# Attention weights of two key blocks added by heads on GpSimd, one product with ones per pair, and the transfers of the normalisation issued by SyncE

## The reference, cut to what matters

```python
scores = jnp.einsum('bhqd,bhkd->bhqk', qn, kn) / jnp.sqrt(jnp.asarray(hd, x.dtype))
scores = jnp.where(causal, scores, jnp.finfo(scores.dtype).min)
w = jax.nn.softmax(scores, axis=-1)
a = jnp.einsum('bhqk,bhkd->bhqd', w, v)
```

## Time and profile before

| | us |
|---|---|
| median of 3 runs | 2458.92 (2458.35 to 2460.32) |
| profiled execution, its own time | 2456.73 |
| its span | 2454.6 |
| TensorE busy in the span | 2279.7 (93%) |
| attention stage, steady part | 487 to 1165 of the span, a unit every 47.3 |

### The profile page before, as it was taken

One profiled execution on the slowest core, in us unless ns is written; L12 is line 12 of the kernel. 1 busy time (PEld: TensorE's weight loads), 2 busy tenths in 40 slices (PEclk: granted clock), 3 DMA queues, 4 the chain that ended last, 5 costly groups with the idle time before them and its releaser, 6 DMA issues. The chain is left out here.

```text
span 2454.6 us, 32466 instructions
## 1 busy us (share of the span) xinstructions
PE 2279.7 (93%) x12520; PEld 1705.3 (69%) x12520; DVE 1165.7 (47%) x1799; ACT 793.3 (32%) x1671; POOL 728.3 (30%) x694
## 2 busy tenths in 40 slices
PE   6999992899999999999858799999999999999998
PEld 3777771666666666666446588888888888888887
DVE  5999994655555555555269611222222212121222
ACT  3333331255555555455435411111111111111111
POOL 2677674002112111111177122222222222222221
PEclk8999996699999999999989899999999999999999
DMA  6122224554465455443179511212121212111111
GB/s 223 69 103 90 98 98 120 122 128 117 102 149 126 106 135 139 111 102 89 37 244 308 204 48 52 69 48 69 52 69 49 68 53 68 44 58 49 48 56 52
DMA packets 161828, 243.70 MB, mean 99 GB/s; under 512 B 17124, under 2 KB 84292, under 8 KB 161184
## 3 DMA queue, kind: packets, MB, share of 16 engines
q1 hardware_dynamic: 153184, 220.66, 30.9%
q0 software_dynamic: 7456, 18.07, 2.5%
q10 hardware_dynamic: 1056, 3.15, 0.3%
HBM read 131.69 MB, written 59.26 MB: 78 GB/s over the span
## 5 line engine op out<-in xcount | busy, mean ns | idle before, releaser
L883 DVE TENSOR_REDUCE b_top<-b_psA 128x2 f32<-128x1024 f32 (+3 forms) x384 | 353.3, 954 | 246.0 <-PE b_psA L801 154.3
L950 ACT ACTIVATE b_probT<-b_psB 128x512 f32<-128x512 f32 (+3 forms) x768 | 338.7, 488 | 330.0 <-PE b_psB L825 242.3
L1313 DVE TENSOR_TENSOR f_gu<-f_psU,f_silu 128x512 f32<-128x512 f32 x128 | 88.5, 691 | 711.8 <-PE f_psU L1380 711.8
L1269 POOL TENSOR_SCALAR f_wd_hi<-f_wd 128x512 fp32r<-128x512 f32 x128 | 83.7, 654 | 822.5 <-PE f_psD L1365 775.6
L822 PE MATMUL b_psB<-b_stack 98*128 98x512 f32 (+3 forms) x768 | 268.2, 404 | 5.0 <-ACT b_probT L950 4.6
L801 PE MATMUL b_psA<-b_stack 96*128 96x512 f32 (+3 forms) x768 | 228.3, 387 | 30.2 <-DMA b_stack<-b_halves 20.3
L822 PEld LDWEIGHTS b_psB<-b_stack 98*128 98x128 f32 x768 | 140.6, 189 | 143.5 <-issue 99.8
L1289 ACT ACTIVATE f_silu<-f_psG 128x512 f32<-128x512 f32 x128 | 76.5, 598 | 503.8 <-PE f_psG L1380 503.8
L1378 PE MATMUL f_psG<-f_hT_hi,w_hi 128*128 128x512 f32 x512 | 200.2, 391 | 10.9 <-DVE f_hT_lo L1307 10.9
L1380 PE MATMUL f_psG<-f_hT_lo,w_hi 128*128 128x512 f32 x512 | 199.7, 390 | 0.0
L1379 PE MATMUL f_psG<-f_hT_hi,w_lo 128*128 128x512 f32 x512 | 199.7, 390 | 0.0
(11 more groups left out here) (177 smaller groups left out, 4136.2 us busy)
## 6 DMA issues: line engine op xcount, KB each, us to landing
b_stack<-b_halves SPq DMA_DIRECT2D x192, 256.0 KB, 5.1
f_wd<-in_wd_t SPq DMA_DIRECT2D x128, 256.0 KB, 2.6
qkv_d<-a_t SPq DMA_DIRECT2D x32, 512.0 KB, 2.7
b_land<-qkv_d SPq DMA_DIRECT2D x32, 512.0 KB, 4.6
a_x<-in_x SPq DMA_DIRECT2D x32, 256.0 KB, 3.2
qkv_d<-a_v SPq DMA_DIRECT2D x32, 256.0 KB, 3.0
b_v<-qkv_d SPq DMA_DIRECT2D x16, 512.0 KB, 5.9
att_d<-b_att SPq DMA_DIRECT2D x16, 512.0 KB, 3.2
```

Of the source, the lines that this page charges most:

```text
L883: dve.tensor_reduce(out, slot("score", NI * n + i)[:, :, 0:width], AX.X, ALU.max, negate=True).then_inc(s["maxed"], 1)
L950: act.activation(probT[:, (NW * n + w) % 3, j, 0:width], psB[:, i % 2, 0:width], ACT.Exp).then_inc(s["expd"], 1)
```

## The change

Per pair of blocks (0 and 1, 2 and 3, ...) GpSimd adds the second block's weights into the first's, head by head; TensorE then makes one product with ones per pair, three steps after the pair's second block was shifted. `b_probT` gets 5 buffers. The transfers of the normalisation move from GpSimd to SP, into the units after, as do the reciprocal (w = 8 to w = 0 of the next unit), the scaling (to w = 3 of the next unit, in two halves) and the store of b_att (from w = 10 of unit g+2 to w = 5 of unit g+3, for group g). Only this much of the diff matters for the order of the work:

```diff
+    PROBS = 5
+    def pair_at(k):
+        at = shift_at(k)
+        return (at[0], at[1] // 2) if at and at[1] % 2 == 1 else None
+    def sum_at(k):
+        return pair_at(k - 3)
+    def take_sum_at(k):
+        return take_at(k - 2)
...
+            def sums_out(n):
+                sp.wait_ge(s["taken_l"], 2 * n + 2)
+                sp.dma_start(scratch["sums"][0], sums[0:P:HD, n % 2]).then_inc(s["sums_out"], 16)
+            def few_in(n):
+                sp.wait_ge(s["sums_out"], 16 * n + 16)
...
+            def few_out(n):
+                sp.wait_ge(s["inverted"], n + 1)
...
+            def wide_in(n):
+                sp.wait_ge(s["few_out"], 16 * n + 16)
...
                 if w == 5 and 0 <= n < NG:
                     load_v(n)
-                if w == 10 and 0 <= n - 2 < NG:
-                    store(n - 2)
+                if 0 <= n - 2 < NG - 1:
+                    if w == 9:
+                        sums_out(n - 2)
+                    if w == 10:
+                        few_in(n - 2)
+                if 0 <= n - 3 < NG - 1:
+                    if w == 1:
+                        few_out(n - 3)
+                    if w == 2:
+                        wide_in(n - 3)
+                if w == 5 and 0 <= n - 3 < NG:
+                    store(n - 3)
...
+            def add_pair(n, i):
+                half, kb = BLOCKS[2 * i + 1]
+                width = (half + 1) * W - max(kb, half * HALF) * P
+                at = (NW * n + 2 * i) % PROBS
+                whole_at = (half + 1) * W - max(kb - 1, half * HALF) * P
+                pool.wait_ge(s["weighed"], NW * n + 2 * i + 1)
+                for j in range(4):
+                    into = probT[:, at, j, whole_at - width:whole_at]
+                    pool.wait_ge(s["expd"], 4 * (NW * n + 2 * i + 1) + j + 1)
+                    add = pool.tensor_tensor(into, into, probT[:, (at + 1) % PROBS, j, 0:width], ALU.add)
+                add.then_inc(s["added"], 1)
...
             for k in STEPS:
                 if prep_at(k):
                     high(*prep_at(k))
-                at = take_at(k)
-                if at and at[1] == 1 and at[0] < NG - 1:
-                    normalise(at[0])
+                if pair_at(k):
+                    add_pair(*pair_at(k))
+                n, w = unit(k)
+                if w == 3 and 0 <= n - 3 < NG - 1:
+                    normalise(n - 3)
...
+            def add_up(n, i):
+                half, kb = BLOCKS[2 * i]
+                pe.wait_ge(s["added"], NW // 2 * n + i + 1)
+                if kb == 0:
+                    at_least(pe, s["taken_l"], 2 * n + half)
...
                 if weigh_at(k):
-                    weigh(*weigh_at(k), False)
-                    weigh(*weigh_at(k), True)
+                    weigh(*weigh_at(k))
+                if sum_at(k):
+                    add_up(*sum_at(k))
...
                 if j == 0:
-                    at_least(act, s["summed"], NW * n + w - 2)
-                    at_least(act, s["weighed"], NW * n + w - 2)
+                    before = NW * n + w - PROBS
+                    if before % 2 == 0:
+                        at_least(act, s["summed"], before // 2 + 1)
+                    else:
+                        at_least(act, s["added"], before // 2 + 1)
+                        at_least(act, s["weighed"], before + 1)
```

More of the change, by code:

```diff
@@ L653, in attention_stage @@
         peak_rows = sb("b_peak_rows", [8 * TB, P])
-        probT = sb("b_probT", [P, 3, 4, W])
+        probT = sb("b_probT", [P, PROBS, 4, W])
         sums = sb("b_sums", [P, 2, C])
@@ L663, in attention_stage @@
         names = ("mask_in ln_ready whole ident_ready consts k_ones qk_in v_in turned hi_done lo_done scored maxed peaks_ready "
-                 "peaks_turned peaks_copied peaks_in shifted expd weighed summed taken_o taken_l sums_out few_in inverted few_out "
+                 "peaks_turned peaks_copied peaks_in shifted expd weighed added summed taken_o taken_l sums_out few_in inverted few_out "
                  "wide_in scaled end_inverted end_scaled").split()
@@ L718, in store @@
                 sp.dma_start(dst, att[:, n % 2].rearrange("p (t q) -> p t q", q=P)).then_inc(stored, 16)
+            def sums_out(n):
[3 more added lines that the diff above has]
+                sp.wait_ge(s["sums_out"], 16 * n + 16)
+                sp.dma_start(few[:, 0], scratch["sums"][0].rearrange("j (a c) -> (j a) c", c=C // HD)).then_inc(s["few_in"], 16)
+            def few_out(n):
+                sp.wait_ge(s["inverted"], n + 1)
+                sp.dma_start(scratch["sums"][1].rearrange("j (a c) -> (j a) c", c=C // HD), few[:, 1]).then_inc(s["few_out"], 16)
+            def wide_in(n):
+                sp.wait_ge(s["few_out"], 16 * n + 16)
+                for j in range(4):
+                    sp.dma_start(sums[j * HD:(j + 1) * HD, n % 2], scratch["sums"][1, j:j + 1].broadcast_to([HD, C])).then_inc(s["wide_in"], 16)
             load(0)
@@ L753, in high @@
                 pool.tensor_scalar(halves[:, 3 if m else 0], whole[:], 1.0, 1.0, ALU.mult, ALU.mult).then_inc(s["hi_done"], 1)
-            def normalise(n):
[L756 to L764, removed]
+            def add_pair(n, i):
[4 more added lines that the diff above has]
+                pool.wait_ge(s["weighed"], NW * n + 2 * i + 1)
+                for j in range(4):
+                    into = probT[:, at, j, whole_at - width:whole_at]
+                    pool.wait_ge(s["expd"], 4 * (NW * n + 2 * i + 1) + j + 1)
+                    add = pool.tensor_tensor(into, into, probT[:, (at + 1) % PROBS, j, 0:width], ALU.add)
+                add.then_inc(s["added"], 1)
+            def normalise(n):
                 pool.wait_ge(s["wide_in"], 64 * n + 64)
                 pool.wait_ge(s["taken_o"], 2 * n + 2)
-                pool.tensor_tensor(att[:, n % 2], att[:, n % 2], sums[:, n % 2], ALU.mult).then_inc(s["scaled"], 1)
+                for half in range(2):
+                    cols = slice(half * W, (half + 1) * W)
+                    mul = pool.tensor_tensor(att[:, n % 2, cols], att[:, n % 2, cols], sums[:, n % 2, cols], ALU.mult)
+                mul.then_inc(s["scaled"], 1)
             for k in STEPS:
@@ L826, in shift, with weigh @@
                 mm.then_inc(s["shifted"], 1)
-            def weigh(n, w, summing):
+            def weigh(n, w):
                 half, kb = BLOCKS[w]
[L830 to L833, removed]
+                pe.wait_ge(s["expd"], 4 * (NW * n + w) + 4)
+                if w == 0:
+                    pe.wait_ge(s["v_in"], 16 * n + 16)
                 if kb == 0:
-                    at_least(pe, s["taken_l" if summing else "taken_o"], 2 * n + half)
+                    at_least(pe, s["taken_o"], 2 * n + half)
                 first = max(kb, half * HALF)
-                out = psL if summing else psO
                 for j in range(4):
                     rows = slice(j * HD, (j + 1) * HD)
-                    mm = pe.matmul(out[rows, (first - half * HALF) * P:W], ones[:] if summing else v[:, n % 2, kb, rows],
-                                   probT[:, (NW * n + w) % 3, j, 0:(half + 1) * W - first * P],
+                    mm = pe.matmul(psO[rows, (first - half * HALF) * P:W], v[:, n % 2, kb, rows],
+                                   probT[:, (NW * n + w) % PROBS, j, 0:(half + 1) * W - first * P],
                                    start=(kb == 0), stop=(kb == (half + 1) * HALF - 1), skip_group_check=True)
-                mm.then_inc(s["summed" if summing else "weighed"], 1)
+                mm.then_inc(s["weighed"], 1)
+            def add_up(n, i):
[3 more added lines that the diff above has]
+                    at_least(pe, s["taken_l"], 2 * n + half)
+                first = max(kb, half * HALF)
+                for j in range(4):
+                    mm = pe.matmul(psL[j * HD:(j + 1) * HD, (first - half * HALF) * P:W], ones[:],
+                                   probT[:, (NW * n + 2 * i) % PROBS, j, 0:(half + 1) * W - first * P],
+                                   start=(kb == 0), stop=(kb == (half + 1) * HALF - 2), skip_group_check=True)
+                mm.then_inc(s["summed"], 1)
             for k in STEPS:
@@ L922, in _ @@
                     low(*prep_at(k))
-                at = take_at(k - 5)
-                if at and at[1] == 1 and at[0] < NG - 1:
-                    dve.wait_ge(s["few_in"], 16 * at[0] + 16)
+                n, w = unit(k)
+                if w == 0 and 0 <= n - 3 < NG - 1:
+                    dve.wait_ge(s["few_in"], 16 * (n - 3) + 16)
                     dve.reciprocal(few[:, 1], few[:, 0]).then_inc(s["inverted"], 1)
-                at = take_at(k)
+                at = take_sum_at(k)
                 if at and at[0] == NG - 1:
@@ L946, in exponent @@
                 if j == 0:
[L947 to L948 removed]
+                    before = NW * n + w - PROBS
[4 more added lines that the diff above has]
+                        at_least(act, s["weighed"], before + 1)
```

(7 more changed lines are left out.)

## The result

The changed kernel took **2670.9 us** in the median (2667.9 to 2673.3), against 2459.1 for the kernel before in the same rounds: ratio 1.086, 95% interval 1.084 to 1.088. The direction was as forecast and the late store is there, but the loss is 212 us where 110 were forecast, and the time lies outside the range: over half of the miss is a cost that the forecast had put at nothing.

A forecast was written before the change was run, and what follows sets the result against it. TensorE, busy 93% of the span, was taken to bound the kernel: 2456.7 (profiled) - 66 for its removed products + 176 for the late store = 2567, plus 2.2 for the median: 2569. Range 2503 to 2612.

The forecast's parts named there:

- TensorE's part: Products with ones of the second blocks removed from TensorE: 4.14 us a unit, a gain of 66 us over 16 groups.
- GpSimd's additions, "hidden": Additions on GpSimd: 22 us a unit, GpSimd busy 27 of 43 us, all covered, so no cost.
- the late store with its clock: Store of b_att delayed on SP: 13.1 us stall plus 1.6 for the clock, 14.7 in 12 units, 176 us.
- that SP reaches the store behind stacks and b_v: In SP's queue the store of b_att is issued only after 12 stacks and b_v, 14.9 us after the burst starts.
- when it lands: The store of b_att lands 21 us after the burst of stacks starts, between 18.1 and 22.8.
- who waits for it: VectorE's copy that frees b_psO waits for the store, and TensorE's product of block 4 waits for that copy.
- 12 units: The stall occurs where there is both a burst of stacks and a store: units 3 to 14.
- its idle time: TensorE idle at block 4's product: 13.1 us, from T + 8.9 to T + 22.0, T being the stack burst's start.
- The rival of a full gain: The store lands in time or VectorE's wait is met otherwise; only TensorE's gain counts: 2393 us, chance 0.09.
- The rival "GpSimd becomes the bound": Additions take half as long again beside VectorE, GpSimd 38 of 43 us: at most 2600 us, chance 0.03.
- the product of 128x1024 at 2.38 us: Evidence against GpSimd slowing: 15 such products on GpSimd already run beside VectorE's row maxima at 2.38 us.
- 3.2 us at the lower level, of which half is lost: TensorE's clock after each stall, taken from the feed-forward start: 1.6 us lost a unit, bounds 0 and twice that.

The follow-up runs named there:

- 2410.7: Changed kernel, three buffers of b_att, GpSimd's additions waiting for the gathered maxima (w = 11) or `low` (w = 1, 3): 2410.7 us, ratio 0.981.
- 2458.6: The kernel before, unchanged, timed beside the follow-up runs: medians 2457.6 to 2458.7 us.
- 2466.6: Changed kernel with three buffers of b_att, so VectorE's copy waits for the store of the group three before: 2466.6 us, ratio 1.0033.
- the late store alone: Kernel of 2410.7 with two buffers of b_att again: 2612.3 us.
- the 38 repeats: Changed kernel with the first score product of w = 7 repeated 38 times per head in units 3 to 14: 2636.9 us.
- Where TensorE still had its products with ones: Kernel before with only SP's part (transfers, reciprocal, scaling, store moved; no additions): 2647.8 us, ratio 1.076; with three buffers of b_att 2465.3.

## Why the prediction was right and where it was wrong

| step of the prediction | forecast, us | measured, us | from |
|---|---|---|---|
| TensorE's part, all else out of the way | -66 | -48 | 2410.7 against 2458.6 |
| GpSimd's additions, "hidden" | 0 | +56 | 2466.6 against 2410.7 |
| the late store with its clock | +176 | +204 | 2670.9 against 2466.6 |
| sum | +110 | +212 | |

**Right:** that SP reaches the store behind stacks and b_v, when it lands (6.7 us after its issue in the median, 3.2 in the kernel before), who waits for it, that it happens in 12 units, and its idle time (12.7 us a unit on average, 9.9 to 13.2, where 13.1 were forecast, by two errors that partly cancel: T + 22.4 for T + 22.0, T + 9.6 for T + 8.9; part of the second is TensorE's wait of 0.78 us at T + 1). The miss of 102 us in the sum is 56 + 28 + 18, all in one direction. The rival of a full gain was wrong in its price: with VectorE's wait met by a third buffer the time is 2466.6, not 2393.

**Wrong: GpSimd's part, put at nothing as "hidden".** This is the step that failed. I costed it by whether GpSimd keeps up. It does: it waited for nothing that matters and the table of waits has TensorE and its weight loads waiting for an addition 3.8 us in all (it is busy 310 us more, where 350 were forecast). What failed is the direction in which the contention was read. The rival "GpSimd becomes the bound" took the contention as a loss of GpSimd, "within its slack", and priced only `low`. The loss that counts was VectorE's, and VectorE's short operations stand on the way to the peaks and to the slots of the scores. The evidence quoted against it, the product of 128x1024 at 2.38 us beside the row maxima, showed the wrong pair: the maxima read b_psA, and they keep 1.22 us in every kernel here. The Trainium skill (GPSIMD Engine Reference, "Specifications") names instructions with two SBUF inputs and those in a 2-port mode. The traces agree for the first kind: `low` and b_least (0.19 to 0.94) have two SBUF inputs, the maxima have none. The cast of b_peaks has one and is held up as well (0.18 to 0.93); in which mode it ran no trace shows. The prediction took `low` for the only operation of that kind on VectorE; two of the three gathering operations are of it too, and I had left them out because each takes 0.2 us. Beside an addition they took the addition's length, not their own.

**A term mis-sized: the clock.** "3.2 us at the lower level, of which half is lost" was 8.4 to 10 us behind the stalls of the changed kernel. The late store costs 204 / 12 = 17.0 us a unit there, of which 12.7 are idle and 4.3 the clock (4.0 by the late store alone, 3.5 net by the 38 repeats): above the bound of twice the value, 3.2. The start of the feed-forward stage was a poor model: there products of 512 columns follow the idle time without a gap, here short steps. Where TensorE still had its products with ones the clock cost 2.4 a unit, nearer to the forecast; that density is the reason is argued, not shown. Not in the sum at all were the clock's dips after the waits of 0.8 and 1.6 us. The waits and these dips together are the +56: 2.5 us a unit of idle and 1.2 of clock, 3.7 of the 4.1 by which the bursts are further apart.

**A term mis-sized: TensorE's gain.** I took a sum's price as the distance from its start to the start of what follows, 0.97 us. A product with v that has no sum behind it shows the flaw; timeline of the kernel of 2410.7:

```profile
679.91 1.06 PE L890 MATMUL b_psO<-b_probT,b_v 128*32 128x512 f32 x8
680.91 0.50 PE L874 MATMUL b_psB<-b_stack 98*128 98x512 f32 x1
...
683.48 1.07 PE L890 MATMUL b_psO<-b_probT,b_v 128*32 128x512 f32 x8
684.36 1.04 PE L902 MATMUL b_psL<-b_probT,b_ones 128*32 128x512 f32 x8
685.33 0.44 PE L874 MATMUL b_psB<-b_stack 98*128 98x384 f32 x1
```

From product to shift it is 1.00 us without a sum and 1.85 with one: a sum of 512 columns is worth 0.85. The 0.12 is paid once, whether a sum or a product with v stands in front of the shift; I read it as the change from products in four 32-column strips (with v, with ones) to whole-array products (shifts, scores). With 0.12 off each, a unit gains 2 x (0.85 + 0.64 + 0.22) = 3.4 us and not 4.14, and 3.2 were measured (47.3 - 44.1). A sum between score and shift has a change on either side of it, which fits its 1.09 us for 0.85. The remaining 0.2 fits the longer waits of weight loads for exponentials (42.3 us against 12.4 before, in 410 us), but was not separated.

**Open:** why waits this short let the clock down, and only some of them. The runs show that either wait suffices and what it costs, not the rule behind it. And how VectorE and GpSimd take turns was seen only in the lengths.

## What to carry to other kernels

A place in an engine's program is not a time: before moving a transfer behind a burst on the same queue, add up what that burst holds and ask who waits for the transfer one buffer turn later. Work handed to GpSimd must be checked for what VectorE does beside it, its shortest SBUF operations first, and a wait for those operations ahead of the additions can be worth more than the additions themselves. Price a removed product by a step that lacks it, not by the distance to the next start; and expect a new wait on a TensorE that had none to cost more than its length: 0.8 us cost 3.5 a unit here, 1.6 cost 3.6, and 12.9 cost 16.9.

## What the runs showed of the hardware that I had not expected

- VectorE's SBUF operations of 0.18 to 0.19 us take 0.93 to 0.95 us beside GpSimd additions of 0.97; `low` goes from 1.23 to 1.75 on average and 2.31 at worst shown; row maxima from b_psA keep 1.22. The additions lengthen too beside `low`: three of 384 columns take 3.91 us, where four take 3.88 beside the gathering.
- Idle stretches of TensorE of 3.2, 3.5 and 12.75 us were each followed by products at the lower of the two levels (1.93 or 1.94 us for 1.07); so were 9 of 11 waits of 0.77 us among short products, but only 1 of 11 of the same waits in the kernel where a wait of 1.59 us stood in each unit as well.
- Filling the idle time with 38 repeated products a head made the kernel 34 us faster while VectorE's wait for the store stayed.
- A product of 512 columns in four 32-column strips takes 0.88 us from start to start when another such product follows, and 1.00 when a whole-array product does.
